# Routed experts in slots ranked by their row count, and a joined matmul for high and low rows

## The reference, cut to what matters

```python
def layer(x):                                        # x: 625 nodes x 512, 20000 edges sorted by dst
    # attention over the edges of each node
    h = layer_norm(x, g, b); q, k, v = split(h @ Wqkv + bqkv)          # 8 heads of 64
    a = einsum('ehd,ehd->eh', q[src] * D**-0.5, k[dst]) + edge_attr_8 + edge_attr_8_n2
    sa = softmax of a over the edges with the same dst
    agg = segment_sum(v[src] * sa, dst);  h1 = node_feature + agg @ Wo + bo
    x = x + h1 + gelu(layer_norm(h1) @ W1 + b1) @ W2 + b2
    # mixture of experts, 8 experts of 512 -> 1024 -> 512, the two best for each row
    xt = layernorm(x); scores = xt @ gate_w.T
    _, idx = top_k(scores + biases, 2);  topv, _ = top_k(scores, 2)
    p = sigmoid(topv) / sum(sigmoid(topv))
    y_e = (silu(xt @ w1[e]) * (xt @ w3[e])) @ w2[e]
    return x + sum_k p[k] * y_idx[k] + (silu(xt @ sw1) * (xt @ sw3)) @ sw2
```

## Time and profile before

| | us |
|---|---|
| time, median of 3 runs | 868.16 (867.26 to 869.63) |
| the profiled execution, its own time | 868.55 |
| its span, first to last instruction | 866.9 |
| mean granted TensorE clock | 0.962 of full speed |
| PE busy | 793.6 |
| DVE busy | 547.8 |
| ACT busy | 439.5 |
| POOL busy | 183.7 |

### The profile page before, as it was taken

The page is one execution under the profiler, slowest core; times in us unless marked ns, Lnnn a source line. Parts: engine busy times, 40 slices in busy tenths (PEclk is TensorE's granted clock), DMA queues, the critical chain, the costliest instruction groups (busy, mean ns, idle before and its releaser), DMA issues. The chain is left out here.

```text
span 866.9 us, 14506 instructions
## 1 busy us (share of the span) xinstructions
PE 793.6 (92%) x5533; PEld 676.0 (78%) x5533; DVE 547.8 (63%) x938; ACT 439.5 (51%) x685; POOL 183.7 (21%) x156
## 2 busy tenths in 40 slices
PE   3996899999999978799997899799999999999993
PEld 2653677787777764699996799699999999999992
DVE  6537998989898935444225544466666666675635
ACT  4244686868686843634342442244545445445420
POOL 9140654545554530000000004000000000000022
PEclk9999899999999989799999799889999999999997
DMA  8320900000000007000002914276756757745024
GB/s 274 100 46 6 365 22 2 1 2 1 2 2 1 2 1 255 0 1 1 1 1 79 388 45 160 78 234 197 237 187 221 249 186 231 228 163 162 22 64 140
DMA packets 64105, 94.39 MB, mean 109 GB/s; under 512 B 6483, under 2 KB 39861, under 8 KB 63525
## 3 DMA queue, kind: packets, MB, share of 16 engines
q1 hardware_dynamic: 61797, 87.74, 30.6%
q0 software_dynamic: 2240, 5.76, 2.2%
HBM read 81.35 MB, written 12.13 MB: 108 GB/s over the span
## 5 line engine op out<-in xcount | busy, mean ns | idle before, releaser
L658 DVE TENSOR_SCALAR onehot<-iota_n,records 128x640 fp32r<-128x640 f32 x160 | 137.0, 879 | 4.0 <-PE ps L776 4.0
L1536 DVE TENSOR_TENSOR w_lo<-weights_far,w_hi 128x1024 fp32r<-128x1024 f32 x64 | 78.3, 1225 | 33.8 <-ACT w_hi L1627 33.8
L1639 ACT ACTIVATE hT<-ps 128x224 f32<-128x224 f32 x64 | 22.9, 358 | 129.9 <-PE ps L1706 129.9
L643 POOL TENSOR_TENSOR bias_exp_hi<-edge_exp_hi,mask 128x640 fp32r<-128x640 f32 x40 | 60.8, 1519 | 119.3 <-DVE mask L663 94.0
L1706 PE MATMUL ps<-xT_hi,w_hi 128*128 128x224 f32 x512 | 79.1, 277 | 3.5 <-DVE w_lo L1536 3.5
L1706 PE MATMUL ps<-xT_lo,w_hi 128*128 128x224 f32 x512 | 79.0, 277 | 0.0
L1706 PE MATMUL ps<-xT_hi,w_lo 128*128 128x224 f32 x512 | 78.8, 276 | 0.0
L1706 PEld LDWEIGHTS ps<-xT_hi,w_hi 128*128 128x128 f32 x512 | 70.9, 195 | 7.0 <-issue 3.8
L776 PE MATMUL ps<-onehot,bias_exp_hi 128*128 128x320 f32 x400 | 70.0, 322 | 6.8 <-DVE onehot L658 6.8
L1522 POOL DMA_INDIRECT weights_far<-slot_results,gate x5 | 4.8, 959 | 303.4 <-DMA slot_results<-weights_near 302.2
L1706 PEld LDWEIGHTS ps<-xT_lo,w_hi 128*128 128x128 f32 x512 | 68.6, 195 | 0.0
(11 more groups left out here) (261 smaller groups left out, 1674.6 us busy)
## 6 DMA issues: line engine op xcount, KB each, us to landing
weights_far<-in_L_ffn_w SPq DMA_DIRECT2D x56, 512.0 KB, 5.6
weights_near<-in_L_ffn_w SPq DMA_DIRECT2D x28, 512.0 KB, 3.6
weights_near<-in_L_gnn_W SPq DMA_DIRECT2D x1, 4096.0 KB, 14.6
weights_far<-in_L_ffn_w SPq DMA_DIRECT2D x2, 2048.0 KB, 19.8
slot_rows<-zeros SPq DMA_DIRECT2D x1, 3584.0 KB, 23.2
vs<-slot_rows SPq DMA_DIRECT2D x8, 448.0 KB, 6.9
slot_results<-weights_near SPq DMA_DIRECT2D x16, 224.0 KB, 5.9
weights_near<-in_L_gnn_Wqkv SPq DMA_DIRECT2D x3, 1024.0 KB, 7.7
```

What stands on the lines that cost most here:

```text
L643: pool.tensor_tensor(to.rearrange("p t (h d) -> p t h d", h=H), e[:, b, :, :].unsqueeze(3).broadcast_to([P, CT, H, BN]), m.unsqueeze(2).br ...
L658: dve.tensor_scalar(onehot[b % 2][:, t, :], iota_n[:, :], rec[:, b, t, 0:1], None, ALU.is_equal).then_inc(oh_ready, 1)
L1536: dve.tensor_tensor(to[1], frm, to[0], ALU.subtract).then_inc(w_lo_ready, 1)
L1639: act.activation(gated[m][:, 0:CAP], psum[2 * m][:, 0:CAP], ACT.Silu).then_inc(a_sb, 1)
```

## The change

1. **Ranks and slots.** The experts are ranked by count with an added DVE chain; rank r has 240 - 16r slots (240 down to 128, 1472 in place of 1792), in blocks of up to 128, so the last rank has one block. The ids of the ranks go to `most[1:9]`, and SP loads weights by id, for rank 0 only after the ranks are known; the rows are read back behind them.
2. **Joined matmul.** `up` takes the high weights by high and low rows side by side in one matmul of 2c columns, then the low weights by the high rows in one of c columns: 16 + 16 matmuls a unit in place of 48. The two column ranges of a bank are added afterwards: ACT copies the second (`low_part`), DVE adds (`parts_summed`), ACT's gate and DVE's product work from SBUF.
3. **w2's low part** is made by POOL, not DVE.
4. **Order on DVE**: `results(r-1)` stands behind `hidden(v, 0)` of unit 1.
5. **The loops** over pairs of experts are written out.
6. **Tail**: DVE combines tiles 0 and 1 between the shared expert's steps and makes the five final adds at the end.
7. **Attention**: 628 node columns in place of 640; the mask of eight blocks in one operation; onehots 0 and 1 in one TENSOR_TENSOR; POOL waits also for the onehots of the block before; PE's first two blocks wait tile by tile.
8. **Blocks**: `attention` and `attention_any`, and `experts_routed` and `experts_all`, share a program block each.

The diff, cut to its core and without changes of indentation:

```diff
@@ constants
-BLK = 112
-CAP = CB * BLK
+CAP = 240
+STEP = 16
+CAPS = [CAP - STEP * r for r in range(EX)]
+FIRST = [sum(CAPS[0:r]) for r in range(EX + 1)]
+SLOTS = FIRST[EX]
+SRC = 2 * (-(-N // 4) * 2)
+SH = SRC // 2
+def slot_blocks(r):
+    return [(s, min(P, CAPS[r] - s)) for s in range(0, CAPS[r], P)]
@@ attention, POOL
-                    pool.wait_ge(masked, b + 1)
+                pool.wait_ge(masked, b // BPT + 1)
+                if b:
+                    pool.wait_ge(oh_ready, (CT - 1) * b)
@@ attention, DVE
+            def onehot_pair(b):
+                wait_past(dve, w_ready, b - 1)
+                dve.tensor_tensor(onehot[b % 2][:, 0:2, :],
+                                  iota_n[:, 0:SRC].unsqueeze(1).broadcast_to([P, 2, SRC]),
+                                  rec[:, b, 0:2, 0:1].broadcast_to([P, 2, SRC]), ALU.is_equal).then_inc(oh_ready, 2)
...
+            masks(0)
                 for b in range(2):
-                    masks(b)
                     onehots(b, range(CT - 1))
                 for b in range(NB):
                     if b + 2 < NB:
-                        masks(b + 2)
-                        onehots(b + 2, (0, 1))
+                    onehot_pair(b + 2)
...
+                if b % BPT == 0 and b // BPT + 1 < NT:
+                    masks(b // BPT + 1)
@@ routing, DVE
+            o.link(dve.scalar_tensor_tensor(out=key, in0=count, scalar=float(EX), in1=behind, op0=ALU.mult, op1=ALU.add))
+            o.link(dve.tensor_tensor(among, key.unsqueeze(1).broadcast_to([P, EX, EX]),
+                                     key.unsqueeze(2).broadcast_to([P, EX, EX]), ALU.is_gt))
+            o.link(dve.tensor_reduce(rank, among, AX.X, ALU.add))
+            o.done(dve.tensor_scalar(first_slot, rank, -STEP / 2, CAP + STEP / 2, ALU.mult, ALU.add))
...
+            o.done(dve.tensor_copy(most[0:1, 1:1 + EX], order[0:1, :]))
@@ experts, SP
+def load_expert(sp, most, r, weights, raw, raw_in):
+    e = sp.snap(sp.value_load(most[0:1, 1 + r:2 + r], min_val=0, max_val=EX - 1))
+    for u in range(UNITS):
+        load_unit(sp, e, u, weights, raw, raw_in)
@@ experts, POOL
+            for v in range(V + 1):
+                u = v % UNITS
+                pool.wait_ge(w_hi_ready, 3 * v + 3)
+                pool.tensor_tensor(w2s[u][1], raw_rest[2] if v == V else raw[u][2], w2s[u][0], ALU.subtract)\
+                    .then_inc(w2_lo_ready, 1)
@@ experts, DVE
+            def parts_summed(v, m):
+                cap = CAPS[v // UNITS]
+                dve.wait_ge(a_low, v * UM + m + 1)
+                dve.tensor_tensor(pair(v, m), pair(v, m), banks[:, 2 * m:2 * m + 2, 0:cap], ALU.add).then_inc(a_sum, 1)
...
+            for v in range(V):
+                r, u = v // UNITS, v % UNITS
+                weights_lo(v + 1, 0)
+                parts_summed(v, 0)
+                weights_lo(v + 1, 1)
+                hidden(v, 0)
+                if u == 1 and r:
+                    results(r - 1)
+                parts_summed(v, 1)
+                if u == 2 and r + 1 < EX:
+                    rows_lo(r + 1)
+                hidden(v, 1)
+                low_hidden(v)
@@ experts, ACT
+            def low_part(v, m):
+                cap = CAPS[v // UNITS]
+                act.wait_ge(a_ps, v * UM + m + 1)
+                wait_past(act, h_made, (v - 1) * UM + m + 1)
+                act.activation(pair(v, m), banks[:, 2 * m:2 * m + 2, CAP:CAP + cap], ACT.Copy).then_inc(a_low, 1)
...
+                weights_hi(v + 1, 0)
+                low_part(v, 0)
+                weights_hi(v + 1, 1)
+                gate(v, 0)
+                low_part(v, 1)
+                weights_hi(v + 1, 2)
+                gate(v, 1)
+                if u == 2 and r + 1 < EX:
+                    rows_hi(r + 1)
+                high_hidden(v)
@@ experts, PE
-                            for i, (wp, xp) in enumerate(passes):
                                 for c in range(DC):
-                                    last = pe.matmul(psum[2 * m + n][:, 0:CAP], w[u % 2][wp][:, c, m * P:(m + 1) * P],
-                                                     xT[k][xp][:, c, :], start=i == 0 and c == 0,
-                                                     stop=i == 2 and c == DC - 1)
+                            pe.matmul(both(bank, cap), w[u % 2][0][:, c, cut], xT(r)[:, c, :, :], start=c == 0, stop=False)
+                        for c in range(DC):
+                            last = pe.matmul(bank[:, 0:cap], w[u % 2][1][:, c, cut], xT(r)[:, c, 0, :], start=False,
+                                             stop=c == DC - 1)
...
+            def down(v):
+                r, u = v // UNITS, v % UNITS
+                pe.wait_ge(h_lo, v + 1)
+                pe.wait_ge(w2_lo_ready, v + 1)
+                for blk, (s0, rows) in enumerate(slot_blocks(r)):
+                    if u == 0 and r:
+                        pe.wait_ge(y_sb, Y_DONE[r - 1] + blk + 1)
@@ tail, DVE
+            rest_hidden(1, 0)
+            combine(0)
+            rest_hidden(1, 1)
+            combine(1)
                 rest_low(1)
+            for t in range(2, NT):
+                combine(t)
                 for t in range(NT):
                     n = P if t < NT - 1 else LAST
                     dve.wait_ge(rest_y, t + 1)
+                dve.tensor_tensor(xs[0:n, t, :], xs[0:n, t, :], rest_out[t][0:n, :], ALU.add).then_inc(summed, 1)
```

More of the change, by code:

```diff
@@ new lines, in sums, with logits, turn @@
+                if part:
+                    last.then_inc(w_ready, 1)
+            def logits(b):
+                wait_past(pe, e_ready, b)
+                for a in range(2):
+                    for c in range(DC):
+                        last = pe.matmul(psum[4 + a][c * 2 * BN:(c + 1) * 2 * BN, 0:SH], KB[:, c, b, :],
+                                         qT[:, c, a * SH:(a + 1) * SH], start=True, stop=True)
+                last.then_inc(s_ready, 1)
+            def turn(b):
+                pe.wait_ge(p_ready, b + 1)
+                wait_past(pe, pt_ready, b)
+                if b % BPT == 0:
+                    wait_past(pe, o_moved, b // BPT)
+                for t in range(NT):
+                    n = min(P, SRC - t * P)
+                    last = pe.transpose(psP[0:n, t, :], PR[b % 2][:, t * P:t * P + n], ident[:, :])
+                last.then_inc(p_turned, 1)
@@ new lines, in weighted_sums @@
+            def weighted_sums(j):
+                pe.wait_ge(pt_ready, BPT * (j + 1))
+                for pair in range(H // 2):
+                    for t in range(NT):
+                        for odd in range(2):
+                            h, r = 2 * pair + odd, slice(DH * odd, DH * (odd + 1))
+                            n = P if t < NT - 1 else LAST
+                            last = pe.matmul(psO[r, pair * P:(pair + 1) * P], vs[0:n, t, h * DH:(h + 1) * DH],
+                                             PT[0:n, t, h, :], start=t == 0, stop=t == NT - 1)
+                last.then_inc(o_ready, 1)
@@ L822, in feed_forward @@
+            for b in range(NB):
+                sums(b, 0)
+                if b % BPT == 1 and b > 1:
+                    weighted_sums(b // BPT - 1)
+                sums(b, 1)
+                logits(b)
+                if b:
+                    turn(b - 1)
+            turn(NB - 1)
+            weighted_sums(NT - 1)
 def feed_forward(nc, sem, finished, x, W2, rows_b, rows_c, wo, w_near, w_far, xs, hT, vs, work, small, ident, psum):
@@ L1780, in experts_all @@
+def experts_all(nc, block, sem, w_in, w1, w3, w2, sw1, sw3, sw2, out, slots, big, xs, hT, work, gate_sb, most, psum):
     gates = gate_views(gate_sb)["gates"]
@@ new lines, in _, with expert @@
+    @block.scalar
+    def _(act):
+        fullest = act.value_load(most[0:1, 0:1], min_val=0, max_val=NP)
+        with act.If(fullest > CAP):
+            def expert(e, chunks=HC):
+                for i in range(2 * chunks):
+                    wait_past(act, a_ps, e * (2 * HC) + (i + 1))
+                    wait_past(act, b_sb, e * (2 * HC) + (i - 1))
+                    act.activation(gated[i % 2], psum[2 * (i % 2)][:, 0:HALF], ACT.Silu).then_inc(a_sb, 1)
+            for k in range(2):
+                expert(k)
+            with act.Fori(1, EX // 2) as j:
+                for k in range(2):
+                    expert(j * 2 + k)
+            expert(EX, UM)
@@ L1894, in attention_any @@
+def attention_any(nc, block, sem, rec_d, qT, KB, PT, hT, vs, iota_n, ident, ones, tab, small, psum, banks):
     with ExitStack() as stage:
@@ L2124 @@
+    'L0_ffn_sw3', 'L0_ffn_sw2']
 def kernel(**inputs):
```

1508 lines of the change are left out of this document (710 added, 798 removed).

## The result

The changed kernel takes 855.65 us (854.59 to 857.25) against 868.36 us for the kernel before, measured beside it; the ratio is 0.9855, with a 95% interval of 0.9834 to 0.9875. It is faster by 12.7 us. 25 us were forecast (843.0, range 831 to 859). On the profiled executions the span falls from 866.9 to 854.0 us. The forecast had the sign, and the range holds the time, but half of the expected gain is missing.

What follows compares the result with a forecast made beforehand. TensorE was taken to bound the routed experts. Attention -10, routed experts -14.4, tail -1.0, block ends -0.6 and start of the experts +0.5 sum to -25.5 on 868.55 us: 843.0, range 831 to 859.

Steps and rivals of the forecast that it cites:

- The price of a matmul: On PE, a joined matmul of 2c columns costs c/1.2 + 13 ns; the low one of c columns stays at 111.6 ns.
- The boundary stall by itself: At seven rank boundaries PE waits for DVE's copy of results, 1.4 to 1.8 us each, 11.1 us in sum.
- POOL's lock: In the routed experts DVE and POOL shut each other out, so POOL's w2 subtraction joins each unit's loop.
- P: Time of POOL's 128x1024 subtraction for w2's low part in each routed-expert unit, taken as 2.3 us.
- the loop of DVE and ACT: Per routed-expert unit, splits, small steps and POOL's subtraction take 3.92 + P + 0.0073c us: 7.97 down to 7.15.
- the larger of this and TensorE's own time: Each routed-expert unit takes the longer of the loop and TensorE's work; ranks sum to 60.5, times 4 is 242.1 us.
- 7 x 1.3 (part of the stall lies in the loop's slack): Rank boundaries add 9.1 us to the routed experts' stage, on top of the units' times.
- The likeliest case: Whole kernel: 843.0 us, with the routed experts' stage at 254.3 against 268.8 us; chance 0.60.
- rival (b): Routed experts: full lock at P = 2.6 and PE's stops drop the clock; 853 to 856 us, taken as 855; chance 0.14.
- Attention: Fewer columns, cheaper masks and onehots bring blocks to about 4.8 us: -10 us, bounds -6 and -13.
- Start of the experts: Weights can't be fetched before the routing, which almost uses up their cover: +0.5 us, bounds 0 and +5.
- The tail: Combines run before TensorE is done and five adds follow: -1.0 us, bounds 0 and -1.5.

Runs made afterwards that it cites:

- experiment 7: Kernel of experiment 5 with the joined matmul undone (48 matmuls a unit, no low_part or part sums): 852.42 us, ratio 0.9798.
- experiment 5: Changed kernel with results copied ahead of unit 1's first part sum and product, and w2's low part made by DVE: 825.40 us, ratio 0.9484.
- experiment 2: Changed kernel with w2's low part made by DVE again, the copy of results still behind the product: 838.62 us, ratio 0.9644.
- experiment 4: Changed kernel with nine useless matmuls put before PE's wait for the copy at each of seven boundaries: 847.89 us, ratio 0.9742.
- experiment 3: Changed kernel with POOL subtracting only 16 of 512 columns of each half in 28 of 32 units, nothing given to DVE: 839.86 us, ratio 0.9656.
- experiment 9: Changed kernel with results copied ahead of unit 1's product, and POOL waiting for the unit's second product before subtracting: 841.33 us, ratio 0.9661.
- experiment 8: Changed kernel with the joint onehot split into two TENSOR_SCALAR operations again: 863.78 us, ratio 0.9923.
- experiment 6: Kernel of experiment 5 with 224 slots for every rank in place of 240 to 128: 848.82 us, ratio 0.9758.

## Why the prediction was half right

**The price of a matmul** was right. The floor of 111.6 ns, left as it was for small column counts, is 110.6 at 128 (experiment 7). Without waits the units' starts (experiment 5) are 7.84, 7.64, 7.36, 7.14, 6.90, 6.66 and 5.07 us apart for 224 to 128 slots without a turn; forecast were 7.77, 7.55, 7.34, 7.13, 6.91, 6.70 and 5.10. The stage of 232.7 us compares with 57.8 x 4 + 3.05 - 1.4 = 232.8, where the 1.4 is the last `down`, which lies behind the remainder's first matmul.

**The boundary stall by itself** was right: 10.7 us in seven waits in experiment 2, 11.1 forecast.

**POOL's lock** had the right size. P was 2.3 and is 2.39 us, and the loop of DVE and ACT has the forecast's period: in the rank of 160 slots the low hidden parts of two units end 7.37 us apart (735.60 and 742.97), forecast 7.38.

```profile
735.11 0.49 DVE L1622 TENSOR_TENSOR hidden_lo<-hT,hidden_hi 128x320 fp32r<-128x320 f32 x1 [0.54 <-ACT hidden_hi L1720]
742.48 0.49 DVE L1622 TENSOR_TENSOR hidden_lo<-hT,hidden_hi 128x320 fp32r<-128x320 f32 x1 [0.54 <-ACT hidden_hi L1720]
```

**The first step that failed** is the next one: "the larger of this and TensorE's own time" as the time of every unit, and the boundaries on top at "7 x 1.3 (part of the stall lies in the loop's slack)". PE doesn't take over the loop's time. In the same rank its first matmuls of the same two units are 6.87 us apart:

```profile
725.68 0.74 PE L1784 MATMUL ps<-xT,w_hi 128*128 128x320 f32 x4
732.55 0.74 PE L1784 MATMUL ps<-xT,w_hi 128*128 128x320 f32 x4
```

PE wants a unit's low hidden part only a whole `up` later, so DVE can fall behind it without stopping it. At the boundary PE wants the copy, and the copy stands behind a product that is late: at 160 slots this product ends 4.33 us behind the first half of `up`, in experiment 2 2.92 us. The 1.41 us between them are just the difference of the two waits, 3.02 and 1.61, and so it is at all seven boundaries. While PE stands, DVE catches up. The 10.7 us became 21.0; with the 3 us elsewhere the lock and the boundaries cost 24.2 us against 20.1 forecast (242.1 - 231.1 = 11.0 for the loop and 9.1). The sum was nearly right, but it came as seven stops of 2.3 to 3.6 us.

**The term that was mis-sized is the clock.** The likeliest case had it at nothing, although it knew no row for the clock behind such stops; rival (b) had one fall at 3 us. There were five, worth 7.8 us in the trace, and experiment 4 takes them back. This follows from the first error: with the stops about as forecast (experiment 2) there is one fall. Rival (b), at 0.14 and "853 to 856", came nearest, by luck in part: the clock fell, but five times at 1.55 us and not once at 3, and P was not 2.6.

In sum, counted to the remainder's first matmul as in the table above, the forecast's stage is 254.3 - 1.4 = 252.9 us and the measured one 264.7. Of the 11.8 us between them 7.8 are the clock and some 4 the waits: the missing half of the gain.

**The rule of the Trainium skill**, "SBUF — State Buffer", section "Who interferes with whom", was borne out in kind: DVE's operations with two inputs in SBUF stand still while POOL reads, here to POOL's end (experiments 2, 3 and 9). The forecast counted the part sums among them; these read one operand from PSUM and are not held up:

```profile
739.40 2.37 POOL L1581 TENSOR_TENSOR w_lo<-weights_far,w_hi 128x1024 fp32r<-128x1024 f32 x1 [5.01 <-ACT w_hi L1699]
740.17 0.47 DVE L1614 TENSOR_TENSOR hT<-hT,ps 128x320 f32<-128x320 f32 x1
741.04 0.91 DVE L1618 TENSOR_TENSOR hT<-hT 128x160 f32<-128x160 f32 x1 [0.40 <-ACT hT L1716]
```

Having POOL do this work cost 17 us, not the 9 of the forecast: 10 of them are waits, as forecast, and most of the rest is the clock.

**Attention** was right, -10.05 with the block end against -10.3, of which 0.9 is the shorter wait for PE's sequencer (1.63 us instead of 2.57). The same text ends up to 1.5 us later in other experiments, so the agreement to 0.3 us is luck. The joint onehot alone is worth 3.7 us of it (experiment 8), though POOL's first product now takes 2.5 us instead of 1.5: it starts 0.06 us behind the pair's operation and ends 1.1 us behind it.

**Start of the experts.** `up` begins 4.6 us behind the first transposes as before, so the late weights cost nothing that is seen. That routing took 2.6 us more and the feed-forward 1.2 less can't be put down to the change: from the feed-forward's first matmul to the first transposes it is 229.7 us before and 231.1 after, and in experiments with the same text there 228.3 (experiment 2) to 233.1 (experiment 6).

**The tail** gained 3.8 us instead of 1.0 (1.3 with the second block end). The adds now follow each other (3.08 us for five), and they begin at 846.0, behind the last gather and its combine and not behind PE's last matmul (842.4). The end is 4.9 us behind the last of them, 7.7 before; why the last store lands sooner wasn't tried.

## What to carry to other kernels

A helper engine that is a little too slow doesn't slow each step of the bound engine. It falls behind unseen while its product is wanted a step later, and the delay is paid where something is wanted in the same step: look for the rare consumer (a bank freed once per expert), not for the mean. Before work is moved to POOL, look at what DVE does next: here an operation with two inputs in SBUF stood still to the end of POOL's, and 1.13 us on DVE was cheaper than 2.4 us on POOL beside it. And keep PE's stops short and few: five of the seven stops of 2.3 to 3.6 us took another 1.55 us each by the clock.

## What the runs showed of the hardware

The clock doesn't follow the length of a stop alone. In the changed kernel stops of 2.29 and 2.64 us left it up and 2.79 us brought it down; in experiment 2 a stop of 1.61 us was followed by the lower level, while 1.53, 1.69 and 1.74 us were not; in experiment 3 the one of 1.69 us was, in experiment 9 the one of 1.74. What decides between them wasn't found. PE's timeline of experiment 2 at the stop of 1.61 us shows its matmuls at 0.63 instead of 0.39 us; the clock granted from 729 to 731 us is 0.50:

```profile
727.89 0.47 PE L1801 MATMUL ps<-w_hi,hidden_hi 128*128 128x512 f32 x1 [1.61 <-DVE weights_near L1629]
728.19 0.44 PE L1801 MATMUL ps<-w_lo,hidden_hi 128*128 128x512 f32 x1
728.43 0.63 PE L1801 MATMUL ps<-w_hi,hidden_lo 128*128 128x512 f32 x1
```
